# Group means by 32x32 transposes on VectorE, and convolution taps without their edge column, in a pre-activation convolution on one core

## What is computed

```python
def _L0_conv_ref(x, weight, att_w, att_b):
    pooled = jnp.mean(x, axis=(2, 3))
    att = jax.nn.sigmoid(pooled @ att_w.T + att_b)
    agg_w = jnp.einsum('nk,kocij->nocij', att, weight)
    def conv_one(xi, wi):
        return lax.conv_general_dilated(xi[None], wi, window_strides=(1, 1), padding=[(1, 1), (1, 1)],
                                        dimension_numbers=('NCHW', 'OIHW', 'NCHW'))[0]
    return jax.vmap(conv_one)(x, agg_w)

x = x + _L0_conv_ref(_gn(x), L0_conv_weight, L0_conv_att_w, L0_conv_att_b)
```

## Time and profile before

| | before |
|---|---|
| median of 3 runs | 1393.18 us (1392.3 to 1393.21) |
| profiled execution, its own time | 1391.56 us |
| span of the profiled execution | 1390.0 us |
| mean granted TensorE clock | 0.993 |
| busy: PE, DVE, ACT, POOL | 1297.0, 1190.4, 925.6, 57.3 us |
| DMA | 165.70 MB, mean 119 GB/s |
| first convolution product | 94.40 us after the span's start |

### The profile page before, as it was taken

The page is one execution under the profiler, slowest core; times in us unless marked ns, Lnnn a source line. Parts: engine busy times, 40 slices in busy tenths (PEclk is TensorE's granted clock), DMA queues, the critical chain, the costliest instruction groups (busy, mean ns, idle before and its releaser), DMA issues.

```text
span 1390.0 us, 25354 instructions
## 1 busy us (share of the span) xinstructions
PE 1297.0 (93%) x8808; PEld 731.4 (53%) x8808; DVE 1190.4 (86%) x2006; ACT 925.6 (67%) x1466; POOL 57.3 (4%) x75
## 2 busy tenths in 40 slices
PE   0259999999999999999999999999999999999998
PEld 0125555555555555555555555555555555555554
DVE  3998898889988898988988899888989889898992
ACT  6656776676667677657776666777776577777531
POOL 0000000000000000000000000000000000000000
PEclk9979999999999999999999999999999999999999
DMA  9020555334455434445553344554344455534253
GB/s 366 2 93 1 140 140 140 90 104 112 120 137 141 125 93 118 109 117 140 140 132 82 104 112 132 141 141 119 91 120 111 120 140 140 139 79 129 51 135 120
DMA packets 29373, 165.70 MB, mean 119 GB/s; under 512 B 3360, under 2 KB 3616, under 8 KB 28192
## 3 DMA queue, kind: packets, MB, share of 16 engines
q1 hardware_dynamic: 20288, 113.94, 22.3%
q0 software_dynamic: 8928, 49.78, 21.2%
HBM read 112.33 MB, written 51.38 MB: 118 GB/s over the span
## 4 chain that ended last, share of the span: by engine, by line
PE 73%; DVE 14%; issue 10%; ACT 1%; DVEq 0%; POOL 0%; POOLq 0%; ACTq 0%
PE pM L428 67%; PE pG L403 6%; DVE Us L572 2%; DVE E L562 2%; DVE T L521 2%; DVE T L556 2%; DVE Vs L578 1%; DVE X L637 1%; DVE W L794 1%; DVE X L649 1%; DVE E L547 1%; DVE E L521 1%; DVE TB L630 0%; DVE TA L630 0%; PE pS L389 0%
## 5 line engine op out<-in xcount | busy, mean ns | idle before, releaser
L428 PE MATMUL pM<-Vs,Us 128*128 128x392 f16 x6912 | 1185.4, 332 | 27.2 <-DVE Us L572 14.0
L428 PEld LDWEIGHTS pM<-Vs,Us 128*128 128x128 f16 x6912 | 670.6, 98 | 530.9 <-issue 46.9
L839 ACT CAST Vs<-E 128x784 f16<-128x784 f32 x192 | 157.0, 844 | 167.0 <-DVE E L547 77.1
L521 DVE SCALAR_TENSOR_TENSOR T<-X 128x392 f32<-128x392 f32 x384 | 193.6, 558 | 7.7 <-ACT X L884 7.0
L578 DVE TENSOR_TENSOR Vs<-E,Vs 128x784 f16<-128x784 f32 x192 | 183.3, 970 | 0.7
L867 ACT ACTIVATE X<-pM,small 128x392 f32<-128x392 f32 x128 | 75.1, 587 | 117.7 <-PE pM L428 117.7
L849 ACT CAST Us<-E 128x768 f16<-128x768 f32 x128 | 102.9, 828 | 73.6 <-PE pM L428 41.5
L572 DVE SCALAR_TENSOR_TENSOR Us<-E,Us 128x768 f16<-128x768 f32 x128 | 119.1, 952 | 32.6 <-issue 30.3
L403 PE MATMUL pG<-W,D 128*32 128x512 f16 x1728 | 105.5, 390 | 31.3 <-DVE W L794 31.3
L905 ACT ACTIVATE unused<-X,small 128x784 bf16<-128x784 f32 x128 | 121.4, 949 | 6.3
L547 DVE SCALAR_TENSOR_TENSOR E<-T 128x784 f32<-128x784 f32 x128 | 119.1, 971 | 4.1
(11 more groups left out here) (75 smaller groups left out, 559.7 us busy)
## 6 DMA issues: line engine op xcount, KB each, us to landing
X<-x_dram SPq DMA_DIRECT2D x66, 784.0 KB, 5.5
out_dram<-X SPq DMA_DIRECT2D x64, 784.0 KB, 3.8
X<-x_dram POOLq DMA_DIRECT2D x62, 784.0 KB, 8.3
W<-w_dram SPq DMA_DIRECT2D x6, 1152.0 KB, 18.9
X<-w_dram SPq DMA_DIRECT2D x2, 1152.0 KB, 26.6
attw<-attw_dram SPq DMA_DIRECT2D x1, 128.0 KB, 8.5
small<-attb_dram SPq DMA_DIRECT2D x1, 0.5 KB, 10.2
```

The costliest lines, as they stand in the source:

```text
L428: mm = pe.matmul(tile_rows(bank(k, o)), Us[:, j, a, c, o, kx, :], v_in(j, b, c, kx), start=(at < 2 and n == 0), stop=(n == 3 * KS * CT - 1 ...
L521: ins = dve.scalar_tensor_tensor(out=dst[c], in0=a[c], scalar=scale, in1=d[c], op0=ALU.mult, op1=ALU.add)
L839: act.copy(v_out(j, 0), e_planes(("V", *v))).then_inc(v_hi, 1)
```

## The change

1. **Group means on VectorE.** The channel values stand in the first two columns of a 128x32 tile `col`. A 32x32 transpose brings the 128 channels of a block into rows, a reduction sums them in eights, one operation scales them and writes each sum eight times, and a second transpose brings them back. This is done for the mean and for the spread. `avg` and its two matmuls are gone.
2. **Edge columns.** V has no zero columns: it is stored as 392 contiguous columns. Taps kx = 0 and 2 read and write 55 of the 56 columns of each row; kx = 1 goes first and covers all.
3. **Order.** The logits stand behind group (6,1), the mixing blocks behind (7,1), (8,1) and (9,1). The orders of VectorE and ScalarE and the lists of counts are written anew. `V(0,0,5)` is made at the start of its own epoch and not at the end of the one before; so is one more low part of U on balance. On VectorE `group_shift` follows `channel_stats` directly, `add_rows` of slot 3 moves back (block 1 behind `attention`); on ScalarE one norm stands ahead of the exponential and three behind it, and `sums(1,0)` stands between the takes (3,0) and (3,1).

```diff
-VW = W + 1
-VROW = TR * VW + 3
+COLS = ((1, W), (0, W), (0, W - 1))
+KX = (1, 0, 2)
...
-        Vs = sb("Vs", [P, NC, 2, CT, VROW], F16)
+        Vs = sb("Vs", [P, NC, 2, CT, U], F16)
...
         def v_in(j, part, c, kx):
-            return Vs[:, j, part, c, kx:kx + TR * VW].rearrange("p (t w) -> p t w", w=VW)[:, :, 0:W]
+            first, last = COLS[kx]
+            return tile_rows(Vs[:, j, part, c, :])[:, :, first + kx - 1:last + kx - 1]
...
-            def group_mean_mm(e):
-                pe.wait_ge(mean_ready, e + 1)
-                pe.matmul(pS[:, 0:CT], avg[:, :], mv[:, :, 0], start=True, stop=True).then_inc(group_mean, 1)
-
-            def group_var_mm(e):
-                pe.wait_ge(spread_ready, e + 1)
-                pe.matmul(pS[:, CT:2 * CT], avg[:, :], spread[:, :], start=True, stop=True).then_inc(group_var, 1)
...
                 for c in range(CT):
-                    for kx in range(KS):
+                    for kx in KX:
+                        first, last = COLS[kx]
                         for a, b in ((0, 0), (0, 1), (1, 0)):
-                            mm = pe.matmul(tile_rows(bank(k, o)), Us[:, j, a, c, o, kx, :], v_in(j, b, c, kx),
-                                           start=(at < 2 and n == 0), stop=(n == 3 * KS * CT - 1),
-                                           skip_group_check=True)
+                            mm = pe.matmul(tile_rows(bank(k, o))[:, :, first:last], Us[:, j, a, c, o, kx, :],
+                                           v_in(j, b, c, kx), start=(at < 2 and n == 0),
+                                           stop=(n == 3 * KS * CT - 1), skip_group_check=True)
...
-                if more:
-                    group_mean_mm(e)
                 group(e, 6, 0)
-                if more:
-                    group_var_mm(e)
                 group(e, 6, 1)
+                if more:
+                    logits_mm(e)
                 group(e, 7, 0)
-                if more:
-                    logits_mm(e)
                 group(e, 7, 1)
+                if more:
+                    mix(e, 0)
                 group(e, 8, 0)
-                if more:
-                    mix(e, 0)
...
+            def group_sums(e):
+                step(e, dve.transpose(colT[:, :], col[:, :]))
+                step(e, dve.tensor_reduce(sums8[:, :], eights(colT), AX.X, ALU.add))
+                return sums8[:, :].unsqueeze(2).broadcast_to([P, CI // GS, GS])
...
             def group_shift(e):
-                dve.wait_ge(group_mean, e + 1)
-                step(e, dve.tensor_scalar(nmean[:, :], pS[:, 0:CT], -1.0, None, ALU.mult))
-                step(e, dve.tensor_tensor(off[:, :], mv[:, :, 0], nmean[:, :], ALU.add))
+                dve.wait_ge(mean_ready, e + 1)
+                sums = group_sums(e)
+                step(e, dve.tensor_scalar(eights(colT), sums, -1.0 / GS, None, ALU.mult))
+                step(e, dve.transpose(nmean32[:, :], colT[:, :]))
+                step(e, dve.tensor_tensor(off[:, :], mean, nmean, ALU.add))
                 step(e, dve.tensor_tensor(sq[:, :], off[:, :], off[:, :], ALU.mult))
-                dve.tensor_tensor(spread[:, :], sq[:, :], mv[:, :, 1], ALU.add).then_inc(spread_ready, 1)
+                step(e, dve.tensor_tensor(spread, sq[:, :], own[:, :], ALU.add))
 
             def group_variance(e):
-                dve.wait_ge(group_var, e + 1)
-                dve.tensor_scalar(var[:, :], pS[:, CT:2 * CT], EPS, None, ALU.add).then_inc(var_ready, 1)
+                sums = group_sums(e)
+                step(e, dve.tensor_scalar(eights(colT), sums, 1.0 / GS, EPS, ALU.mult, ALU.add))
+                dve.transpose(var32[:, :], colT[:, :]).then_inc(var_ready, 1)
```

More of the change, by code:

```diff
@@ L163, in conv_kernel @@
         unused = sb("unused", [P, CR * W // 2], mybir.dt.bfloat16)
-        mv = sb("mv", [P, CT, 2], F32)
-        nmean = small[:, 28:30]
+        mean = col[:, 0:CT]
+        spread = col[:, 0:CT]
+        nmean = nmean32[:, 0:CT]
+        var = var32[:, 0:CT]
+        own = small[:, 28:30]
         rstd = small[:, 30:32]
@@ L312, in conv_kernel, with dve_count @@
         assert sorted(LAST) == sorted(DVE_TAKES)
-        assert LAST[:ND - 3 * CT] == DVE_TAKES[:ND - 3 * CT]
-        def last_count(takes):
-            return N * ND + max(LAST.index(t) for t in takes) + 1
+        def dve_count(e, takes):
+            order = LAST if isinstance(e, int) and e == N else DVE_TAKES
+            return e * ND + max(order.index(t) for t in takes) + 1
         block = ctx.enter_context(nc.Block())
@@ L351, in last_epoch @@
                     sp.wait_ge(x_summed, 3 * CT)
-                    sp.wait_ge(dve_took, last_count([("rows", 9, o), ("edge", 10, o), ("edge", 11, o)]))
+                    sp.wait_ge(dve_took, dve_count(N, [("rows", 9, o), ("edge", 10, o), ("edge", 11, o)]))
                     store(N, b, CH - 1, o)
@@ L584, in channel_stats @@
                 step(e, dve.tensor_reduce(total[:, :], s1[:, :, :], AX.X, ALU.add))
-                step(e, dve.tensor_scalar(mv[:, :, 0], total[:, :], 1.0 / (H * W), None, ALU.mult))
-                step(e, dve.tensor_tensor(off[:, :], mv[:, :, 0], nk[:, :], ALU.add))
+                step(e, dve.tensor_scalar(mean, total[:, :], 1.0 / (H * W), None, ALU.mult))
+                step(e, dve.tensor_tensor(off[:, :], mean, nk[:, :], ALU.add))
                 step(e, dve.tensor_tensor(sq[:, :], off[:, :], off[:, :], ALU.mult))
@@ L655, in add_x @@
                 dve.wait_ge(x_beside[o], 16)
[L656 removed]
+                dve.wait_ge(dve_took, dve_count(N, [("rows", 9, o)]))
                 q = CR * (CH - 1) + 1
@@ L704, in epoch @@
+                take_edge(e, b, 5, 1)
+                v_low(e, (0, 1, 0))
+                add_rows(e, b, 3, 0)
                 v_low(e, (0, 1, 4))
                 if more:
-                    norm_scale(e)
-                v_low(e, (0, 1, 5))
-                take_edge(e, b, 5, 1)
+                    attention(e)
                 add_rows(e, b, 3, 1)
-                v_low(e, (0, 1, 0))
                 if more:
-                    attention(e)
                     v_pair(e, 1 - b, ("V", 1, 0, 1))
@@ L917, in epoch @@
             def epoch(e, b, more):
-                u_high(e, (0, 1, 1))
-                u_high(e, (0, 0, 3))
                 u_high(e, (0, 0, 0))
-                if more:
-                    sums(e, 1 - b, 0, 0)
-                u_high(e, (0, 0, 5))
                 u_high(e, (0, 1, 3))
@@ L949, in epoch @@
                 if more:
-                    root(e)
-                v_high(e, (0, 1, 5))
-                take_first(e, 6, 0)
-                if more:
-                    norm(e, 1 - b, 0, 1)
-                    norm(e, 1 - b, 1, 1)
                     norm(e, 1 - b, 1, 0)
@@ L958, in epoch @@
                     norm(e, 1 - b, 0, 0)
+                    norm(e, 1 - b, 1, 1)
+                    norm(e, 1 - b, 0, 1)
+                take_first(e, 6, 0)
+                take_first(e, 6, 1)
+                if more:
+                    v_high(e, (1, 0, 1))
+                    take_taps(e, 0)
+                    take_taps(e, 1)
+                    take_taps(e, 2)
                 take_first(e, 7, 0)
                 take_first(e, 7, 1)
-                take_first(e, 6, 1)
                 if more:
-                    take_taps(e, 0)
-                    take_taps(e, 1)
+                    v_high(e, (1, 0, 3))
                 take_pair(e, b, 8, 0)
                 if more:
-                    take_taps(e, 2)
-                    v_high(e, (1, 0, 3))
-                    v_high(e, (1, 0, 1))
                     v_high(e, (1, 0, 2))
                     take_taps(e, 3)
+                    take_taps(e, 4)
                 take_pair(e, b, 8, 1)
-                if more:
-                    take_taps(e, 4)
                 take_pair(e, b, 9, 0)
```

219 lines of the change are left out of this document (106 added, 113 removed), and 8 rows, old and new, of the table E_ITEMS.

## The result

| | before | after |
|---|---|---|
| median | 1392.74 us (1390.88 to 1393.21) | 1361.74 us (1361.27 to 1362.60) |
| ratio | | 0.9781, 95% interval 0.9764 to 0.9797 |
| span of the profiled execution | 1390.0 us | 1359.2 us |
| first convolution product | 94.40 us | 95.96 us |

The account below looks back on a forecast made before the run. Bound: TensorE's stream plus one late hand-over per pass. Terms -4.0 - 13.4 - 5.5 + 0.8 - 1.1 = -23.2 us take the profiled 1391.56 to 1368.4; the median, 1.6 above, 1370.0 us; range 1362 to 1380.

Parts of the forecast that it names:

- Term 1: TensorE's stream, epochs 1 to 15: the two fp32 products for means go, 0.27 us an epoch, -4.0 us.
- Terms 2 and 3: Convolution products: outer taps lose seven columns, 2.9 ns each, -13.4 us; the middle tap reads one contiguous run, -5.5 us.
- rival A: Outer taps lose the 2.4 ns excess as well, 11.1 us more off TensorE; about 1362 us, chance 0.13.
- rivals B and D: Broken output rows in outer taps eat the columns' gain, about 1380 us (0.10), or cost more, 1399 us (0.05).
- One sign of being wrong: Outer taps: the prediction would be wrong if 385 columns take as long as 392.
- Term 4: VectorE's new transposes and sums: 1.4 us more an epoch, covered in the loop; prologue +0.8 us.
- It is covered: VectorE in the loop: the added 1.4 us an epoch fits, since it no longer waits 3.2 us for the exponential.
- Term 5: New order: late hand-over per pass stays, 1.6 us instead of 1.7, moved to "other" (2,1) at group (4,1); -1.1 us.
- until its jump (5.60): VectorE's chain from pair V(1,0,1): works until a back-edge jump of 5.60 us, 62.9 us in all before the change.
- short jumps, on time: Term 5, end of its range: with short jumps "other" (2,1) is on time; -7.8 us.
- Prologue, +0.8: VectorE's new steps, uncovered before the all-reduce: 1.4 us less 0.7 of waiting for the second mean, +0.8 us.

Follow-up runs that it names:

- The two steps measured one by one: Kernel with new order and means, all columns, 1378.8 us; then outer taps cut to 55 columns with V still in rows of 57, 1371.25 us.
- the means alone: The kernel before with only the group means moved to VectorE, old order and all columns: 1399.15 us, ratio 1.0058.
- The experiment that brings the long jump back: The changed kernel with V(0,5) made last in the epoch before, not first in its own, so VectorE's jump falls later: 1369.1 us, ratio 0.9827.

## Why the prediction was right, and where it was short

- **The bound.** Right: TensorE's stream plus one late hand-over per pass, and the gap at the back edge is TensorE's own jump. The loop written out shows both.
- **Term 1**, means off TensorE, -4.0: right, 0.27 us an epoch.
- **Terms 2 and 3**, -13.4 and -5.5: together 1.19 us an epoch forecast, 1.10 measured, 17.6 us. The sum was near, but by luck: both terms were mis-sized, one each way. The prediction gave all taps one spacing before (168.6 to 169.0 ns), but the middle tap took 169.6 and the outer ones 168.2. So an outer product gained 2.10 ns and not 2.9 (4608 of them: -9.7), and a middle one 3.43 and not 2.4 (2304 of them: -7.9). The two steps measured one by one say the same: 0.49 us an epoch for the columns, where 0.84 were forecast, and 0.61 for the layout, where 0.35 were.
- **The outer taps** keep the cost of a broken row, as forecast: rival A is out, although its 1362 us is where the time came to lie. The reason was too narrow, since broken output costs the same as broken input, and a break alone is not free: seven runs cost 2.5 ns, where I had read nothing from two runs in the earlier trace rows. It didn't show in the outer taps, as their input was broken anyway, and so rivals B and D fell too. One sign of being wrong did come up by its letter: 385 columns in seven runs (166.1 ns) take as long as 392 in one run (166.2). Against 392 in seven runs they save 2.1.
- **Term 4**, 1.4 us an epoch: right in size. "It is covered" was right for the new order only. In the old one it lies on the chain, as the means alone show.
- **Term 5, the order, -1.1: this failed.** The lateness (7.8 us as waits, 9.2 by the starts of the epochs) went altogether. The step that failed is "until its jump (5.60)": I carried the old jump into the new chain, and it takes 1.4 (3.2 once). The rest of the chain was near: the start 47.9 against 48.8 (the table for the exponential is loaded while the logits are still being waited for), "other" (2,1) as the first thing to be late, due at 106.4 against 106.6. The experiment that brings the long jump back has that wait, and 1369.1 us, against my 1370.0. The range had this case in it ("short jumps, on time"; end -7.8), but I called it an end of a range and didn't ask what sets the length of a jump, though the earlier trace rows had one of 3.6 beside those of 5.6.
- **Prologue, +0.8.** The first product is 1.6 us later (1.2 to 1.6 later than in the three runs that have the prologue of before): 0.75 by VectorE's steps (the first mixing product at 61.66, before at 60.91), the rest in the mixing, where TensorE ran at the lower of its two clock levels for longer (72 products in 6.95 us, before in 5.76). The clock gives it back: in the first group it rises earlier, 4.48 us against 5.75 for 18 products. Neither was forecast, and neither is firmly the change's: the kernel before written out has the same prologue, and its first group took 4.31.
- **The sum.** -4.0, -17.6, -9.4 and, for the prologue with the first group, +0.3 (1.6 - 1.3) come to -30.7; measured -30.8 on the span. The forecast was 7.6 short of that, and term 5 alone is 8.3 of it.

## What to carry to other kernels

A small product or a small step costs what it makes others wait: price it in the order in which it will stand, since the same edit was worth -28 us in one order and +8 in the other. An engine's jump at a loop's back edge is work with a price that changes with the transfers under way; let it fall ahead of them, or write the loop out, before moving work around it. When a stall is carried over into a new schedule, ask what sets its length.

## What the runs showed of the hardware

- VectorE's jump back took 1.3 to 1.7 us (once 2.1) where its branch came ahead of the issue of the accumulating transfer, 2.5 without that transfer, and 3.1 to 6.0 where the branch came behind the issue. Each time VectorE restarted some 2 us after a load of 8 KB on the instruction queue began. TensorE stood idle 0.6 to 1.2 us at its own jump in all kernels with a loop.
- 385 fp16 columns from one run into one run start 163.3 ns apart. Seven runs on the input, or on both sides, cost the same tap 165.8; seven on the output alone cost the other outer tap the 166.4 that it takes with both. The Trainium skill's rule of columns at 2.4 GHz plus 2.5 ns (TensorE: Matmul & The Clock Gate, section "Wait — 56ns, not 53.3ns?") gives 162.9 and agrees with the first. That a non-contiguous pattern in PSUM "slows matmuls significantly" (PSUM — Partial Sum Buffer, section "Specifications (TRN2)") comes to 1.5% here, the same as on the input side.
- In rows of 57 the middle tap took 169.6 ns in the kernel before and 169.9 between outer taps of 55, against 168.2 for the outer taps of before with the same number of runs and columns. The three taps start at elements 0, 1 and 2 of a row; that the odd start costs the 1.4 ns was not tested.
